# Two value products in every second step: reordering the slots of a cross attention on the matrix engine

## The chip, the core and the metric

The kernel runs on one core of a Trainium2 chip, in one launch. Its matrix engine (TensorE, PE in the profile) writes only to PSUM, eight banks of 512 columns of float32; VectorE (DVE) and ScalarE (ACT) read PSUM, GpSimd (POOL) works on SBUF, and SyncE (SP) issues the transfers. Each engine takes its instructions in the order in which they are written and waits for semaphores. The metric is the device time of one execution in microseconds.

## What is computed

A model of two layers on x of 16 x 64 tokens, width 128. Each layer adds a cross attention to a context of 16 x 1601 keys, a self attention, and a mixture of experts. The change touches the cross attention of layer 1 alone, with 16 heads of width 8:

```
q = split_heads(layernorm(x) @ cq_w + cq_b)
k = split_heads(ctx @ ck_w + ck_b)          # ctx: [16, 1601, 128]
v = split_heads(ctx @ cv_w + cv_b)
scores = einsum('bqhd,bkhd->bhqk', q, k) / sqrt(8) + mask
probs = softmax(scores, axis=-1)
ca = einsum('bhqk,bkhd->bqhd', probs, v)    # goes on to @ co_w and a normalisation
```

All is in float32, and the softmax takes its maximum away before the exponential.

## The kernel before

The cross attention of layer 1 runs in **slots**, one per batch element n, written by `slot` in each engine's block and unrolled by `slots`: n = -2 to 1, a loop of five rounds of two slots, n = 12 to 16. The 1601 keys are 13 **tiles** of 128 (the last has 65), and a slot has 13 **steps**, k = 0 to 12. In a slot PE works on three batch elements at once:

- **Scores** of tile k for n (`scores`, L1371): four matmuls (in the profile `PS<-QB,KS`, 256 columns each) into banks 2 and 3 or 4 and 5 in turn. They wait until the exponential of tile k - 2 has been taken from these banks.
- ScalarE takes the **exponential** (L1174), 128 x 1024, from PSUM into `PT`, which has two halves, used in turn. It waits until the product of tile k - 2 has read its half.
- **Value product** of tile k (`values`, L1356): eight matmuls, each on 32 columns of the array (`tile_position`), four side by side, in float32 (each makes two records in the profile, `PS<-PT,work_area` or `PS<-PT,early`, so 16 records a product). It accumulates in bank 6. In a step, the product of tile k - 1 follows the scores of tile k; that of tile 12 stands at the head of the next slot.
- **Maximum blocks** (`maximum`, L1333; `PS<-KS,QM`): the scores of batch element n + 1, for their maximum alone, with the queries in the rows. There are 26, m0 to m25, mostly one matmul of 512 columns each into bank 0, 1 or 7; VectorE reduces each (L1583) and so frees its bank. The table `UNITS` says in which step and bank each stands. Then PE transposes the negated maximum (`nm`, L1331), and VectorE takes it as two parts, `nmh` and `nml` (L1593, L1594), in step 11.
- **Side items** through bank 7 (`SIDE`, `beside`): the sum of the softmax (`sum`, step 1), value projections v0 to v3 of element n + 1 (steps 2 to 5), key projections k0 to k3 of element n + 2 (steps 6, 7, 11, 12). ScalarE takes each out of bank 7 (L1141, L1152, L1156). v3 is one tile and k3 65 columns; the others are full. `IN_BANK7` is the order of all users of bank 7; each waits until the one before has been taken out.

GpSimd splits the keys in two parts and spreads the queries (L1022, L1037, L1039), and SyncE stacks the parts in `KS` by transfers. A maximum block waits for the last block in its bank to be reduced, and for its stacked keys.

So the order inside a step of before is: scores k, the blocks, value product k - 1, the side item. In step 0 it is: value product 12 of the slot before, the blocks, scores 0. The order is written out by hand; no planner moves it.

Of the kernel before, what the change touches and what calls it, by code (L numbers as in the profile page):

```python
# [53 lines left out]
def build(nc, A, out, scratch, mask_parts):  # L54
    ctx = ExitStack()
    with ctx:
# [86 lines left out]
        with nc.sbuf_tensor("context2", [128, 2 * KT * 128], F32) as context2:  # L143
# [6 lines left out]
        VA = [value_area.rearrange("p (k h c) -> p k h c", k=KT, h=HEADS // 2),  # L150
              early[:, :].rearrange("p (k h c) -> p k h c", k=KT, h=HEADS // 2)]
        PT = sb("PT", [128, 2, 1024])

        mask_sb = PT[0:BATCH, :, :].rearrange("p a n -> p (a n)")[:, 0:KPAD]
        mask_hi, mask_lo = kh[0:BATCH, :], kl[0:BATCH, :]
# [562 lines left out]
        pieces = [[(p, c)] for p in range(8) for c in (0, 1)] + [[(p, 2)] for p in range(8)]  # L718
        pieces += [[(p, 3) for p in range(7)], [(7, 3)]]
        UNITS = []  # L720
        for k, banks in ((12, (0, 1)), (0, (0, 1, 7)), (1, (0, 1)), (2, (0, 1)), (3, (0, 1)), (4, (0, 1)), (5, (0, 1)),
                         (6, (0, 1)), (7, (0, 1)), (8, (0, 1, 7)), (9, (0, 1, 7)), (10, (0,))):
            UNITS += [(k, bk, pieces[len(UNITS) + j]) for j, bk in enumerate(banks)]
        assert len(UNITS) == len(pieces)
        progress("keys_p", [f"k{c}" for c in CS])
        progress("keys_a", [f"kf{c}" for c in CS])
# [85 lines left out]


        SIDE = {1: "sum", 2: "v0", 3: "v1", 4: "v2", 5: "v3", 6: "k0", 7: "k1", 11: "k2", 12: "k3"}
        IN_BANK7 = ["m4", "sum", "v0", "v1", "v2", "v3", "k0", "k1", "m21", "m24", "nm", "k2", "k3"]
        assert [f"m{m}" for m, (k, bk, _) in enumerate(UNITS) if bk == 7] == ["m4", "m21", "m24"]

        def present(item, n):
            c = isinstance(n, int)
# [3 lines left out]
                return not (c and n > 13)  # L823
            return not (c and (n < -1 or n > 14))

        def maxima(n, k):

            c = isinstance(n, int)
            ahead = 2 if k == KT - 1 else 1
            if c and not 0 <= n + ahead < BATCH:  # L830
                return [], None
            return [m for m, unit in enumerate(UNITS) if unit[0] == k], n + ahead

        def side(n, k):

# [252 lines left out]
        def _(act):  # L1088
# [69 lines left out]
            def slot(n, q):  # L1158
                c = isinstance(n, int)
                for k in range(KT):  # L1160
                    if k == 0 and not (c and n < 1):
                        at(S, "pv_p", f"pv{KT - 1}", n - 1)
                        if not (c and n < 2):
                            at(S, "fin_g", "on", n - 2)
                        P["acc_a"].done(S.activation(acc_sb, bank(6, 256), ACT.Copy), "acc")
                    if not (c and (n < 0 or n > 15)):
                        rows = 128 if k < FULL else TAIL
                        par = (k + q) % 2
                        at(S, "exp_p", f"s{k}", n)
                        if k >= 2:  # L1170
                            at(S, "pv_p", f"pv{k - 2}", n)
                        elif not (c and n < 1):
                            at(S, "pv_p", f"pv{k + KT - 2}", n - 1)
                        P["exp_a"].done(S.activation(PT[0:rows, par, :], PS[0:rows, 1024 + 1024 * par:2048 + 1024 * par],  # L1174
                                                     ACT.Exp), f"e{k}")
                    for item in side(n, k):
                        empty(item, n, q)
# [14 lines left out]
        def _(pe):  # L1192
# [163 lines left out]
            def values(n, k, q):  # L1356
                rows = 128 if k < FULL else TAIL
                at(T, "exp_a", f"e{k}", n)
                if k == 0:
                    at(T, "vals_a", "v3", n)  # L1360
                    if not (isinstance(n, int) and n < 1):
                        at(T, "acc_a", "acc", n - 1)
                for r in range(2):
                    for j in range(4):
                        p = 4 * r + j
                        last = mm(PS[32 * j:32 * j + 32, 3072 + 128 * r:3200 + 128 * r], VA[q][0:rows, k, p, :],
                                  PT[0:rows, (k + q) % 2, 128 * p:128 * p + 128], start=k == 0 and r == 0,
                                  stop=k == KT - 1, skip_group_check=True, tile_position=(0, 32 * j))
                P["pv_p"].done(last, f"pv{k}")

# [13 lines left out]

            def slot(n, q):
                live = not (isinstance(n, int) and (n < 0 or n > 15))
                for k in range(KT):
                    units, batch = maxima(n, k)
                    stack = q if k == KT - 1 else 1 - q
                    if k == 0:  # L1390
                        if not (isinstance(n, int) and n < 1):
                            values(n - 1, KT - 1, 1 - q)
                        for m in units:
                            maximum(m, batch, stack, n)
                        if live:
                            scores(n, k, q)
                    else:
                        if live:
                            scores(n, k, q)
                        for m in units:  # L1400
                            maximum(m, batch, stack, n)
                        if k == 11 and present("nm", n):
                            beside("nm", n, q)
                        if live:
                            values(n, k - 1, q)
                    for item in side(n, k):
                        beside(item, n, q)

            slots(pe, slot)

# [326 lines left out]
```

## Time and profile before

| | |
|---|---|
| three runs | 1234.77, 1239.29, 1239.86 us (median 1239.29) |
| the profiled execution | 1236.02 us, span from first to last instruction 1234.2 us |
| slots of layer 1's cross attention in it | from about 405 to 888 us |
| busy over the span: PE, DVE, ACT, POOL | 1022.8, 651.9, 494.8, 345.9 us |
| mean granted clock of TensorE | 0.907 |
| maximum reductions (L1583) | 416, 665 ns each |
| exponentials (L1174) | 208, 1021 ns each |
| the chain that ended last | PE 74%, DVE 14%, ACT 5% of the span |

The shares say which engine to look at; the slots are more than a third of the span, and what bounds them is read there. A row of the timeline gives the start, the time from the first start to the last end of a merged group, and the count. PE's matmuls are pipelined: the record of one block of 512 columns lasts 0.39 us and the next begins sooner. So a price on PE is a distance between starts.

### The profile page before, as it was taken

The numbers are of one execution on the slowest core, as the hardware profiler recorded it, in microseconds if no ns is written. First come the engines' busy times: TensorE is split into PE (matmuls) and PEld (weight loads), VectorE is DVE, ScalarE is ACT, GpSimd is POOL, SyncE is SP. The second block draws the span as 40 slices with busy tenths as digits, with TensorE's granted clock in tenths as the row PEclk, the third lists the DMA queues.
The fourth block names the chain that finished last, engine by engine and source line by source line (L and its number), as shares of the span: only waits on it lengthen the run. The fifth ranks groups of instructions, "written<-read, shape, count | busy, mean of one in ns | idle before, by whom it ended". The sixth has DMA issues, their size and how long they took to land.

```text
span 1234.2 us, 24027 instructions
## 1 busy us (share of the span) xinstructions
PE 1022.8 (83%) x9486; PEld 759.7 (62%) x9486; DVE 651.9 (53%) x1302; ACT 494.8 (40%) x654; POOL 345.9 (28%) x360
## 2 busy tenths in 40 slices
PE   4998684999983799999999999999757633828998
PEld 3676454888861476767777776677535421527897
DVE  3445567444342556666666666666166368655111
ACT  1444153222220156666565665665515101402443
POOL 0200213112203434444444444443131012110110
PEclk9999795999995799999999999999979766957999
DMA  8786001010302554444444444433000000010211
GB/s 251 183 281 258 1 2 51 27 52 27 105 1 51 135 123 118 113 115 119 114 114 113 108 109 121 122 84 83 2 1 2 0 1 0 2 34 1 52 35 35
DMA packets 54250, 96.95 MB, mean 79 GB/s; under 512 B 15704, under 2 KB 31856, under 8 KB 54176
## 3 DMA queue, kind: packets, MB, share of 16 engines
q1 hardware_dynamic: 54176, 95.90, 28.6%
q8 instruction: 54, 0.88, 0.3%
q14 instruction: 20, 0.16, 0.0%
HBM read 40.97 MB, written 13.84 MB: 44 GB/s over the span
## 4 chain that ended last, share of the span: by engine, by line
PE 74%; DVE 14%; ACT 5%; POOL 3%; DMA 2%; issue 2%; SPq 1%; DVEq 0%; ACTq 0%; POOLq 0%
PE PS L261 68%; PE PS L1209 2%; DVE u_all L274 2%; ACT PT L1174 1%; PE PS L353 1%; PE PS L291 1%; POOL rstd_all L280 1%; ACT work_area L403 1%; DVE stats_all L266 1%; PE PS L1242 1%; DVE work_area L452 1%; DVE smax L451 1%; DMA early<-in_ctx 1%; SPq L957 1%; DVE ctxT L274 1%
## 5 line engine op out<-in xcount | busy, mean ns | idle before, releaser
L1583 DVE TENSOR_REDUCE mx<-PS 128x1 f32<-128x512 f32 (+2 forms) x416 | 256.7, 665 | 162.3 <-PE PS L261 161.9
L1174 ACT ACTIVATE PT<-PS 128x1024 f32<-128x1024 f32 (+1 forms) x208 | 210.6, 1021 | 61.5 <-PE PS L261 60.2
L261 PE MATMUL PS<-QB,KS 128*128 128x256 f32 (+1 forms) x832 | 160.7, 319 | 0.3 <-DMA QB<-nml 0.3
L261 PE MATMUL PS<-QB,QS 128*128 128x512 f32 x576 | 150.9, 411 | 1.1 <-POOL QS L568 0.7
L261 PE MATMUL PS<-KS,QM 128*128 128x512 f32 (+1 forms) x512 | 142.8, 379 | 6.5 <-DMA KS<-kl 5.1
L261 PEld LDWEIGHTS PS<-QB,KS 128*128 128x128 f32 (+1 forms) x832 | 115.2, 186 | 35.4 <-issue 24.8
L261 PEld LDWEIGHTS PS<-QB,QS 128*128 128x128 f32 x576 | 106.2, 193 | 32.5 <-DVE PT L653 5.9
L661 DVE SCALAR_TENSOR_TENSOR x<-PS,tok_w,x 128x128 f32<-128x128 f32 x128 | 36.0, 344 | 119.5 <-PE PS L261 119.5
L261 PEld LDWEIGHTS PS<-KS,QM 128*128 128x128 f32 x512 | 80.3, 192 | 26.0 <-issue 13.0
L291 PE MATMUL PS<-consts,u_all 128*128 128x128 f32 x64 | 15.6, 426 | 90.6 <-DVE u_all L274 70.0
L261 PEld LDWEIGHTS PS<-expert_area,work_area 128*128 128x128 f32 (+2 forms) x1000 | 78.8, 171 | 16.5 <-ACT work_area L406 12.0
L261 PE MATMUL PS<-expert_area,work_area 128*128 128x128 f32 (+3 forms) x1000 | 81.0, 255 | 5.8 <-ACT work_area L406 3.3
L640 ACT ACTIVATE work_area<-PS 128x512 f32<-128x512 f32 x64 | 38.3, 598 | 108.6 <-PE PS L261 108.6
L566 POOL TENSOR_TENSOR QS<-expert_area,consts 128x512 fp32r<-128x512 f32 x24 | 25.0, 1040 | 189.8 <-DMA expert_area<-in_L_ffn_experts_w 106.1
L261 PE MATMUL PS<-ctxT,w_L_xattn_ck_w 128*128 128x512 f32 (+1 forms) x128 | 64.0, 584 | 15.7 <-ACT prT L1152 12.2
L1037 POOL TENSOR_TENSOR kh<-prT,consts 128x512 fp32r<-128x512 f32 x32 | 33.6, 1051 | 141.1 <-ACT prT L1152 141.1
L261 PE MATMUL PS<-PT,work_area 128*32 128x128 f32 (+1 forms) x1664 | 67.0, 279 | 3.3 <-ACT PT L1174 3.1
L291 PEld LDWEIGHTS PS<-consts,u_all 128*128 128x128 f32 x64 | 12.6, 224 | 91.9 <-DVE u_all L274 52.7
L261 PE MATMUL PS<-PT,early 128*32 128x128 f32 (+1 forms) x1664 | 67.0, 279 | 2.3 <-ACT PT L1174 2.3
L261 PE MATMUL PS<-w_L_xattn_cv_w,ctxT 128*128 128x128 f32 (+1 forms) x416 | 63.3, 291 | 0.4 <-ACT work_area L1141 0.4
L261 PEld LDWEIGHTS PS<-expert_area,PT 128*128 128x128 f32 x512 | 59.6, 192 | 1.5
L261 PE MATMUL PS<-expert_area,PT 128*128 128x128 f32 x512 | 59.8, 275 | 0.0
(253 smaller groups left out, 1527.5 us busy)
## 6 DMA issues: line engine op xcount, KB each, us to landing
KS<-kh SPq DMA_DIRECT2D x128, 128.0 KB, 2.4
ctxT<-context_transposed SPq DMA_DIRECT2D x16, 800.5 KB, 4.4
context_transposed<-transposed SPq DMA_DIRECT2D x14, 800.5 KB, 10.1
KS<-kh SPq DMA_DIRECT2D x128, 72.1 KB, 2.1
KS<-kl SPq DMA_DIRECT2D x64, 128.0 KB, 2.4
context<-in_ctx SPq DMA_DIRECT2D x8, 768.0 KB
expert_area<-in_L_ffn_experts_w SPq DMA_DIRECT2D x24, 256.0 KB, 3.1
KS<-kl SPq DMA_DIRECT2D x64, 72.1 KB, 2.1
```

Of the source, the lines that this page charges most:

```text
L261: return T.matmul(o, l, r, start=start, stop=stop, **k)
L266: V.bn_stats(stats_all[:, t, :], src[:, t, :]).then_inc(ln_stats, 1)
L274: V.tensor_scalar(dst[:, t, :], src[:, t, :], mv_all[:, t, 0:1], rstd_all[:, t:t + 1], ALU.subtract, ALU.mult).then_inc(ln_xn, 1)
L280: G.tensor_tensor(rstd_all[:, :], var_all[:, :], minus_half.broadcast_to([128, PAIRS]), ALU.pow).then_inc(ln_rstd, 1)
L291: last = T.transpose(PS[:, 512 * (6 + h) + 128 * t:512 * (6 + h) + 128 * t + 128], src[:, 4 * h + t, :], ident)
L566: P[name + "_g"].done(G.tensor_tensor(hi, w[:, j, :], one.broadcast_to([128, FF]), ALU.mult), f"w{2 * k + 1}hi{e}")
L640: ins = S.activation(g_act[:, c % 2, :], bank(2 * (c % 2)), ACT.Silu)
L661: last = V.scalar_tensor_tensor(x[:, 4 * t + q, :], PS[:, 512 * (4 + t) + q * 128:512 * (4 + t) + (q + 1) * 128], tok_w[:, 4 * t + q, e:e ...
L1037: P["keys_g"].done(G.tensor_tensor(kh[:, c0:c0 + cw], src, one.broadcast_to([128, cw]), ALU.mult), f"kh{m}")
L1174: P["exp_a"].done(S.activation(PT[0:rows, par, :], PS[0:rows, 1024 + 1024 * par:2048 + 1024 * par], ACT.Exp), f"e{k}")
L1209: last = T.transpose(PS[:, 512 * (4 + g % 2) + 128 * j:512 * (4 + g % 2) + 128 * j + rows], ctx_nat[n % 4][0:rows, b, k0 + j, :], consts[0 ...
L1583: P["max_v"].done(V.reduce_max(mx[:, p:p + len(parts), c:c + 1], bank(bk, cw * len(parts)).rearrange("q (p k) -> q p k", k=cw), AX), f"m{m}")
```

## The change

`PTS` is a list of three probability buffers: the two halves of `PT`, and 1024 columns of `expert_area` that nothing else uses at that time. The exponential of tile k goes to `PTS[k % 3]` and waits for the product of tile k - 3. The value products of tiles k - 2 and k - 1 are both written in the even step k; the odd steps have none. The blocks get a place within their step: "start" (step 0, behind the product of tile 12), "scores" (behind the scores) or "values" (at the step's end, behind products and side item), and are spread over steps and places anew. In step 12 the side item k3 stands directly behind the scores, ahead of block m0. Number and size of all matmuls, reductions, exponentials and transfers stay.

```
--- before.py
+++ after.py
@@ -150,6 +150,7 @@
         VA = [value_area.rearrange("p (k h c) -> p k h c", k=KT, h=HEADS // 2),
               early[:, :].rearrange("p (k h c) -> p k h c", k=KT, h=HEADS // 2)]
         PT = sb("PT", [128, 2, 1024])
+        PTS = [PT[:, 0, :], PT[:, 1, :], expert_area[:, 2048:3072]]
 
         mask_sb = PT[0:BATCH, :, :].rearrange("p a n -> p (a n)")[:, 0:KPAD]
         mask_hi, mask_lo = kh[0:BATCH, :], kl[0:BATCH, :]
@@ -718,9 +719,13 @@
         pieces = [[(p, c)] for p in range(8) for c in (0, 1)] + [[(p, 2)] for p in range(8)]
         pieces += [[(p, 3) for p in range(7)], [(7, 3)]]
         UNITS = []
-        for k, banks in ((12, (0, 1)), (0, (0, 1, 7)), (1, (0, 1)), (2, (0, 1)), (3, (0, 1)), (4, (0, 1)), (5, (0, 1)),
-                         (6, (0, 1)), (7, (0, 1)), (8, (0, 1, 7)), (9, (0, 1, 7)), (10, (0,))):
-            UNITS += [(k, bk, pieces[len(UNITS) + j]) for j, bk in enumerate(banks)]
+        for k, place, banks in ((12, "scores", (0,)), (0, "start", (1, 0, 7)), (0, "scores", (1,)), (1, "scores", (0,)),
+                                (2, "scores", (1,)), (2, "values", (0, 1)), (3, "scores", (0,)),
+                                (4, "scores", (1,)), (4, "values", (0, 1)), (5, "scores", (0,)),
+                                (6, "scores", (1,)), (6, "values", (0, 1)), (7, "scores", (0,)),
+                                (8, "scores", (1,)), (8, "values", (0, 1, 7)), (9, "scores", (0, 1, 7)),
+                                (10, "scores", (0,))):
+            UNITS += [((k, place), bk, pieces[len(UNITS) + j]) for j, bk in enumerate(banks)]
         assert len(UNITS) == len(pieces)
         progress("keys_p", [f"k{c}" for c in CS])
         progress("keys_a", [f"kf{c}" for c in CS])
@@ -812,8 +817,8 @@
 
 
         SIDE = {1: "sum", 2: "v0", 3: "v1", 4: "v2", 5: "v3", 6: "k0", 7: "k1", 11: "k2", 12: "k3"}
-        IN_BANK7 = ["m4", "sum", "v0", "v1", "v2", "v3", "k0", "k1", "m21", "m24", "nm", "k2", "k3"]
-        assert [f"m{m}" for m, (k, bk, _) in enumerate(UNITS) if bk == 7] == ["m4", "m21", "m24"]
+        IN_BANK7 = ["m3", "sum", "v0", "v1", "v2", "v3", "k0", "k1", "m21", "m24", "nm", "k2", "k3"]
+        assert [f"m{m}" for m, (k, bk, _) in enumerate(UNITS) if bk == 7] == ["m3", "m21", "m24"]
 
         def present(item, n):
             c = isinstance(n, int)
@@ -823,13 +828,13 @@
                 return not (c and n > 13)
             return not (c and (n < -1 or n > 14))
 
-        def maxima(n, k):
+        def maxima(n, k, place=None):
 
             c = isinstance(n, int)
             ahead = 2 if k == KT - 1 else 1
             if c and not 0 <= n + ahead < BATCH:
                 return [], None
-            return [m for m, unit in enumerate(UNITS) if unit[0] == k], n + ahead
+            return [m for m, unit in enumerate(UNITS) if unit[0][0] == k and place in (None, unit[0][1])], n + ahead
 
         def side(n, k):
 
@@ -1167,11 +1172,11 @@
                         rows = 128 if k < FULL else TAIL
                         par = (k + q) % 2
                         at(S, "exp_p", f"s{k}", n)
-                        if k >= 2:
-                            at(S, "pv_p", f"pv{k - 2}", n)
+                        if k >= 3:
+                            at(S, "pv_p", f"pv{k - 3}", n)
                         elif not (c and n < 1):
-                            at(S, "pv_p", f"pv{k + KT - 2}", n - 1)
-                        P["exp_a"].done(S.activation(PT[0:rows, par, :], PS[0:rows, 1024 + 1024 * par:2048 + 1024 * par],
+                            at(S, "pv_p", f"pv{KT - 1}", n - 1)
+                        P["exp_a"].done(S.activation(PTS[k % 3][0:rows, :], PS[0:rows, 1024 + 1024 * par:2048 + 1024 * par],
                                                      ACT.Exp), f"e{k}")
                     for item in side(n, k):
                         empty(item, n, q)
@@ -1364,7 +1369,7 @@
                     for j in range(4):
                         p = 4 * r + j
                         last = mm(PS[32 * j:32 * j + 32, 3072 + 128 * r:3200 + 128 * r], VA[q][0:rows, k, p, :],
-                                  PT[0:rows, (k + q) % 2, 128 * p:128 * p + 128], start=k == 0 and r == 0,
+                                  PTS[k % 3][0:rows, 128 * p:128 * p + 128], start=k == 0 and r == 0,
                                   stop=k == KT - 1, skip_group_check=True, tile_position=(0, 32 * j))
                 P["pv_p"].done(last, f"pv{k}")
 
@@ -1384,27 +1389,33 @@
 
             def slot(n, q):
                 live = not (isinstance(n, int) and (n < 0 or n > 15))
+
+
+                def block_maxima(k, place):
+                    units, batch = maxima(n, k, place)
+                    for m in units:
+                        maximum(m, batch, q if k == KT - 1 else 1 - q, n)
+
                 for k in range(KT):
-                    units, batch = maxima(n, k)
-                    stack = q if k == KT - 1 else 1 - q
                     if k == 0:
                         if not (isinstance(n, int) and n < 1):
                             values(n - 1, KT - 1, 1 - q)
-                        for m in units:
-                            maximum(m, batch, stack, n)
-                        if live:
-                            scores(n, k, q)
-                    else:
-                        if live:
-                            scores(n, k, q)
-                        for m in units:
-                            maximum(m, batch, stack, n)
-                        if k == 11 and present("nm", n):
-                            beside("nm", n, q)
-                        if live:
-                            values(n, k - 1, q)
-                    for item in side(n, k):
-                        beside(item, n, q)
+                        block_maxima(k, "start")
+                    if live:
+                        scores(n, k, q)
+                    if k == KT - 1:
+                        for item in side(n, k):
+                            beside(item, n, q)
+                    block_maxima(k, "scores")
+                    if k == 11 and present("nm", n):
+                        beside("nm", n, q)
+                    if live and k and k % 2 == 0:
+                        values(n, k - 2, q)
+                        values(n, k - 1, q)
+                    if k < KT - 1:
+                        for item in side(n, k):
+                            beside(item, n, q)
+                    block_maxima(k, "values")
 
             slots(pe, slot)
```

What PE does around steps 2 and 3 (names: `QB,KS` scores, `KS,QM` blocks, `PT` or `expert_area` with `work_area` products, `w_L_xattn_cv_w` value projections), before:

```order
L261 MATMUL PS<-QB,KS 128x256 x4
L261 MATMUL PS<-KS,QM 128x512 x2
L261 MATMUL PS<-PT,work_area 32x128 x8
L261 MATMUL PS<-w_L_xattn_cv_w,ctxT 128x128 x4
L261 MATMUL PS<-QB,KS 128x256 x4
L261 MATMUL PS<-KS,QM 128x512 x2
L261 MATMUL PS<-PT,work_area 32x128 x8
L261 MATMUL PS<-w_L_xattn_cv_w,ctxT 128x128 x4
```

and after:

```order
L262 MATMUL PS<-QB,KS 128x256 x4
L262 MATMUL PS<-KS,QM 128x512
L262 MATMUL PS<-PT,work_area 32x128 x16
L262 MATMUL PS<-w_L_xattn_cv_w,ctxT 128x128 x4
L262 MATMUL PS<-KS,QM 128x512 x2
L262 MATMUL PS<-QB,KS 128x256 x4
L262 MATMUL PS<-KS,QM 128x512
L262 MATMUL PS<-w_L_xattn_cv_w,ctxT 128x128 x4
```

Both products are in step 2 now. Two blocks (7 in bank 0, 8 in bank 1) end it, and block 9, in bank 0 again, comes one score tile later.

PE from step 8 to the transpose of step 11 (the block with 66 columns x7 is m24), before:

```order
L261 MATMUL PS<-QB,KS 128x256 x4
L261 MATMUL PS<-KS,QM 128x512 x3
L261 MATMUL PS<-PT,work_area 32x128 x8
L261 MATMUL PS<-QB,KS 128x256 x4
L261 MATMUL PS<-KS,QM 128x512 x2
L261 MATMUL PS<-KS,QM 128x66 x7
L261 MATMUL PS<-PT,work_area 32x128 x8
L261 MATMUL PS<-QB,KS 128x256 x4
L261 MATMUL PS<-KS,QM 128x66
L261 MATMUL PS<-PT,work_area 32x128 x8
L261 MATMUL PS<-QB,KS 128x256 x4
L1331 MATMUL PS<-consts,nm 8x128
```

and after, from step 8 as well:

```order
L262 MATMUL PS<-QB,KS 128x256 x4
L262 MATMUL PS<-KS,QM 128x512
L262 MATMUL PS<-PT,work_area 32x128 x16
L262 MATMUL PS<-KS,QM 128x512 x3
L262 MATMUL PS<-QB,KS 128x256 x4
L262 MATMUL PS<-KS,QM 128x512 x2
L262 MATMUL PS<-KS,QM 128x66 x7
L262 MATMUL PS<-QB,KS 128x256 x4
L262 MATMUL PS<-KS,QM 128x66
```

Blocks 19 to 24 stand with nothing but one score tile between them.

PE from the transpose of step 11 into the next slot, after (`ctxT,w_L_xattn_ck_w` are key projections k2 and k3):

```order
L1336 MATMUL PS<-consts,nm 8x128
L262 MATMUL PS<-ctxT,w_L_xattn_ck_w 128x512
L262 MATMUL PS<-QB,KS 65x256 x4
L262 MATMUL PS<-ctxT,w_L_xattn_ck_w 128x65
L262 MATMUL PS<-KS,QM 128x512
L262 MATMUL PS<-PT,work_area 32x128 x8
L262 MATMUL PS<-expert_area,work_area 32x128 x8
L262 MATMUL PS<-PT,work_area 32x128 x8
L262 MATMUL PS<-KS,QM 128x512 x3
L262 MATMUL PS<-QB,KS 128x256 x4
L262 MATMUL PS<-KS,QM 128x512
```

Before, a product stood between the transpose and k2, and two blocks and a product between the scores of tile 12 and k3. Now the products of tiles 10, 11 and 12 are neighbours.

## Rows read from the trace of the kernel before

**Rows 1.** Busy time by stretches: before slot 0, two neighbouring slots (from `nm` to `nm`).

```profile
core 0: us, PE busy (x) PEld busy (x) DVE busy (x) ACT busy (x) POOL busy (x), PEclk, DMA share, GB/s
405.00:434.00 29.00, 24.56 (x79) 14.94 (x79) 19.66 (x34) 6.04 (x10) 12.74 (x14) 0.74 0.57 138
603.72:633.25 29.53, 28.95 (x332) 20.68 (x329) 18.51 (x31) 17.76 (x23) 14.13 (x19) 1.00 0.45 113
633.25:662.42 29.17, 28.89 (x331) 20.61 (x329) 18.50 (x31) 17.77 (x23) 14.08 (x19) 1.00 0.46 114
```

**Rows 2.** Timeline of PE, one full step; start, length, engine, line, names, count.

```profile
614.64 0.72 PE L261 MATMUL PS<-QB,KS 128*128 128x256 f32 x4
615.20 0.63 PE L261 MATMUL PS<-KS,QM 128*128 128x512 f32 x2
615.76 0.64 PE L261 MATMUL PS<-PT,work_area 128*32 128x128 f32 x16
616.34 1.16 PE L261 MATMUL PS<-w_L_xattn_cv_w,ctxT 128*128 128x128 f32 x8
617.25 0.71 PE L261 MATMUL PS<-QB,KS 128*128 128x256 f32 x4
```

**Rows 3.** Timeline of PE, heads of two slots, in narrow windows.

```profile
461.55 0.97 PE L261 MATMUL PS<-KS,QM 128*128 128x512 f32 x3
462.35 1.10 PE L261 MATMUL PS<-QB,KS 128*128 128x256 f32 x8
463.29 0.63 PE L261 MATMUL PS<-KS,QM 128*128 128x512 f32 x2
464.09 0.42 PE L261 MATMUL PS<-PT,early 128*32 128x128 f32 x8 [0.17 <-ACT PT L1174]
...
608.52 0.40 PE L261 MATMUL PS<-KS,QM 128*128 128x512 f32 x1
...
608.76 0.39 PE L261 MATMUL PS<-KS,QM 128*128 128x512 f32 x1
```

**Rows 4.** Timeline of PE, one value product, in two windows.

```profile
613.16 0.43 PE L261 MATMUL PS<-PT,work_area 128*32 128x128 f32 x8
...
613.16 0.64 PE L261 MATMUL PS<-PT,work_area 128*32 128x128 f32 x16
```

**Rows 5.** Timeline of DVE, the reduction of the block at 615.20.

```profile
615.63 0.69 DVE L1583 TENSOR_REDUCE mx<-PS 128x1 f32<-128x512 f32 x1 [0.44 <-PE PS L261]
```

**Rows 6.** Timeline ahead of slot 0, reductions of DVE, weight loads of PE behind them.

```profile
422.09 3.76 DVE L1583 TENSOR_REDUCE mx<-PS 128x1 f32<-128x512 f32 x7 [0.62 <-PE PS L261]
...
423.43 0.19 PEld L261 LDWEIGHTS PS<-KS,QM 128*128 128x128 f32 x1 [0.35 <-DVE mx L1583]
424.03 0.97 PEld L261 LDWEIGHTS PS<-KS,QM 128*128 128x128 f32 x8 [0.41 <-DVE mx L1583]
```

**Rows 7.** Timeline of steps 11 and 12, all engines.

```profile
603.72 0.27 PE L1331 MATMUL PS<-consts,nm 128*8 128x128 f32 x1
...
604.35 0.28 DVE L1594 TENSOR_TENSOR nml<-PS,nmh 8x128 fp32r<-8x128 f32 x1
...
604.68 1.12 PE L261 MATMUL PS<-ctxT,w_L_xattn_ck_w 128*128 128x512 f32 x2
...
605.92 0.69 ACT L1152 ACTIVATE prT<-PS,c_L_xattn_ck_b 128x512 f32<-128x512 f32 x1 [0.98 <-PE PS L261]
...
606.11 0.63 PE L261 MATMUL PS<-KS,QM 128*128 128x512 f32 x2
```

**Rows 8.** Timeline at a slot's head, ACT and PE.

```profile
609.74 1.94 ACT L1174 ACTIVATE PT<-PS 128x1024 f32<-128x1024 f32 x2 [0.95 <-PE PS L261]
...
609.93 0.63 PE L261 MATMUL PS<-KS,QM 128*128 128x512 f32 x2
...
611.03 0.64 PE L261 MATMUL PS<-PT,work_area 128*32 128x128 f32 x16 [0.47 <-ACT PT L1174]
```

**Rows 9.** Timeline of PE, step 8.

```profile
627.42 1.04 PE L261 MATMUL PS<-KS,QM 128*128 128x512 f32 x3
...
628.39 0.64 PE L261 MATMUL PS<-PT,work_area 128*32 128x128 f32 x16
```

## Prediction, made before the changed kernel ran

> **What bounds the kernel now.** I read the busy time of each engine by stretches first. The 16 slots of layer 1's cross attention take two lengths in turn, 29.53 and 29.17 us, mean 29.35, with the matrix engine (PE) busy 28.95 and 28.89 us of them at a granted clock of 1.00; VectorE is busy 18.5 and ScalarE 17.8 us [rows 1]. So PE bounds a slot, and only PE's own time, or a wait that PE meets, counts. Next I read PE alone in order of time, to get the price of each item by the distance from start to start (records overlap, so their lengths are too long). Then the places where PE stands next to another engine: banks handed over by VectorE, the chain of the negated maximum, the first exponential of a slot.
>
> **Prices.** Eight score matmul records, two key tiles, take 462.35 to 463.29: 0.47 us per tile. Two maximum blocks start 608.52 and 608.76: 0.23 each [rows 3]. A full step from 614.64 to 617.25 holds one score tile, two blocks, one value product and a value projection of 0.91 (616.34 to 617.25), in 2.61 us. So a lone value product costs 2.61 - 0.47 - 0.46 - 0.91 = 0.77 [rows 2]. Inside one, the first 8 records span 0.43 and all 16 span 0.64, so eight more take 0.21 and sixteen 0.43 [rows 4]. A second product directly behind the first therefore costs 0.43, and a lone one carries 0.34 of change-over. Where a block or side item had to wait, its weight load is no longer hidden: three blocks after a change-over take 461.55 to 462.35 = 0.80, not 0.69 [rows 3]; I price this exposed load at 0.11.
>
> The hand-over of a bank: block at 615.20, its reduction at 615.63, so 0.43 later, for 0.69 [rows 2, 5]. Queued reductions end 0.60 apart (PE's reloads behind them stand at 423.43 and 424.03). The reductions started 422.09, the second thus ends 422.09 + 0.60 + 0.69 = 423.38, and the load that needed it came at 423.43: 0.06 [rows 6]. So a bank can be written again 0.43 + 0.69 + 0.06 = 1.18 after its block, and the new block then moves 0.11 later, at 1.29; the third bank of three adjacent blocks at 1.29 + 1.20 = 2.49.
>
> **Part 1: products together.** Before there are 13 lone value products a slot. After, six runs: tiles 0 and 1, 2 and 3, up to 8 and 9, and then 10, 11 and 12, because the one at the next slot's head follows directly. Seven change-overs go. Six of them are worth 6 x 0.34 = 2.04. The seventh is not a gain. Tile 10's product stood between the transpose of the negated maximum (603.72) and key projection k2 (604.68), and k2 waits for VectorE's second half of that maximum, which starts 604.35 and lasts 0.28 [rows 7]. The chain takes these 0.96 us whatever PE does meanwhile, so 0.77 of work was almost free there, and without it the time stays. Now the product is paid elsewhere: +0.43. Behind the waiting k2 all later items of the slot are queued on PE.
>
> **Part 2: waits that go.** The product of tile 0 waited for the first exponential: 609.93 to 611.03 is 1.10 for two blocks and the change-over, which take 0.56 at 615.20 to 615.76, so 0.54 of waiting; in the other kind of slot 463.29 to 464.09 is 0.80, so 0.24 [rows 2, 3, 8]. Mean 0.39. It now stands a step later, with tile 1's exponential behind it on ScalarE (two in 1.94 us, 609.74 to 611.68), and the sum, a score tile and a block before it: gone. The bank-7 block of step 8 waited for key evacuation: 627.42 to 628.39 is 0.97 for three blocks and a change-over, 0.79 unhindered, so 0.18 [rows 9]; it now stands behind two products: gone. The third probability buffer costs nothing and is needed: the exponential of tile k overwrites tile k-3, whose product ran before its scores were queued.
>
> **Part 3: waits that come.** All are in the new order of blocks and sides.
> - Steps 3, 5 and 7 begin with scores and then a block in bank 0, whose last block (7, 11, 15) ended the step before. Between the two starts PE has two blocks and a score tile, 0.46 + 0.47 = 0.93; the bank is good at 1.29. Waiting 0.36 each, 1.08. Before, a value product and a side item lay between.
> - Blocks 19, 20, 21, one score tile, 22, 23, 24: the products that lay between are gone. Block 24 would start 5 x 0.23 + 0.47 = 1.62 after 19, its bank is good at 2.49: 0.87 for the three.
> - Blocks 1, 2, 3 at the slot's head, then scores, 4, scores, 5, sum. The sum would start 0.69 + 0.47 + 0.23 + 0.47 + 0.23 = 2.09 after block 1, and needs bank 7, good at 2.49: 0.40 (block 4 takes part of the same).
> - k3 now follows the scores directly and needs bank 7 from k2. k2 starts 604.68, ScalarE takes it at 605.92 for 0.69, end 606.61, that is 1.93, with 0.06 and 0.11: 2.10. The scores are over at 606.11, 1.43 after [rows 7]. Waiting 0.67. Blocks 0 and 1 and tile 11's product covered this before. Queued behind: block 0, three products.
>
> Sum: 1.08 + 0.87 + 0.40 + 0.67 = 3.02. None of these is in the trace of before as such; their bounds are nothing (if something I count as idle turns out to be filled) and these values plus 0.11 each.
>
> The Trainium skill, TensorEngine Tiling (PSUM Bottleneck), says that tiling speeds TensorE but not the evacuation of PSUM. That speaks against this change, and by it the sum would stand on the side of the 3.02, as my rows put it.
>
> **Sum.** A slot: -2.04 + 0.43 - 0.39 - 0.18 + 3.02 = +0.84. Thirteen slots (1 to 13) have all of it: +10.9. Slot 0 has no sum item: +0.4. Slots 14 and 15 have no key projections, the last no blocks either, so merging pays and little waits: -1.2 for both, an estimate. Ahead of slot 0, with no scores to cover them, the three waits in bank 0 can be 0.36 + 0.47 = 0.83 each, against waits that stand there already: 0 to 2.5, I take 1.5. Total +11.6. Everything behind the slots is untouched. The profiled execution took 1236.0 us (span 1234.2), so 1247.6; the median of the runs, 1239.3, stands 3.3 above it, by which it is 1250.9. I take 1249.
>
> **Rivals.**
> *The merging pays and the waits stay away (faster).* Only the gains of parts 1 and 2 come: -2.18 a slot, over 14 slots -30.5, so 1208. For it: in before PE shows hardly a wait for VectorE, and VectorE has 11 us of idle time in a slot. Against: it is the distance of two blocks in one bank that counts, and for blocks 7 and 9 that shrinks from a whole step of 2.6 us to 0.93. It decides if a bank is free again within 0.93 of its block instead of 1.18. The Trainium skill, TensorEngine Tiling (Key Properties), says that changing the tiling mode drains the engine; my 0.34 is that drain, and by that rule alone seven would go at 2.4 us a slot.
> *Even.* Only the exposed loads are my error: without 0.11 on six waits (three in bank 0, 24, the sum, k3) a slot gains 0.66 back, 13 x 0.66 = 8.6: 1239 by the profile, 1242 by the median. The rows show this load after a change-over and in a few waits, not in these.
> *The clock.* In the 29 us ahead of slot 0, where PE waits for banks, the mean granted clock was 0.74 (stretches at 1.2 GHz) [rows 1]. A mean of 0.74 over 29 us is 15 us at the lower level, and each such stretch among the slots, where PE bounds, would cost 15 x 0.5 = 7.5. The new order puts 3 us of waits into each slot, but spread in pieces under 1 us, and none of the waits of before inside the slots went with a fall. Two such stretches: 1264.
> *The pair does not run as a run* (0.77 for the second product too): +0.84 + 2.04 a slot, 1275. Rows inside one product speak against it.
>
> **Chances.** Forecast 0.56 (1243 to 1257), even 0.20, faster 0.17, the clock or no run 0.07. The range leaves out the faster rival and the far end: 1230 to 1262. About 0.5% (6 us) is what a measurement of this kernel can tell from no change: faster 0.17, same 0.22, slower 0.61.
>
> **What would show it.** Slots of 30.2 us with the alternation smaller. In PE's order: 0.64 + 0.43 for a pair of products, then the side item. PE waiting for VectorE's reductions about seven times a slot, near nothing before; a key projection k2 0.96 behind the transpose with nothing between; k3 waiting 0.6 for ScalarE; no wait before the product of tile 0. If slots are shorter than 29.2, the banks come free earlier than 1.18 behind their block, or the blocks are further apart than I count, and the forecast is wrong at part 3.

## The result, and the profile after

The changed kernel takes 1254.2 us in the median of four runs (1251.8 to 1255.89), the kernel before 1239.57 (1234.77 to 1240.93): a ratio of 1.0124, 95% interval 1.009 to 1.0157. So it is slower by 15 us. Forecast was 1249 with 1243 to 1257 around it, from a sum of 12 us. The profiled execution of the changed kernel took 1255.6 us, its span is 1253.8.

Where the time came in is read by stretches, cut at the first maximum block and at the transposes `nm` in step 11, from one to the next. First the kernel before, then the changed one (columns as in [rows 1]):

```profile
405.02:426.21 21.19, 18.28 (x64) 11.27 (x65) 16.18 (x27) 3.76 (x7) 7.83 (x9) 0.80 0.52 132
426.21:457.01 30.80, 29.15 (x275) 20.23 (x276) 16.88 (x29) 16.35 (x20) 11.57 (x11) 0.89 0.49 120
457.01:838.14 381.13, 375.83 (x4279) 268.18 (x4277) 240.59 (x403) 230.92 (x299) 181.59 (x223) 1.00 0.46 112
838.14:865.96 27.82, 27.31 (x328) 19.85 (x325) 18.50 (x31) 16.61 (x21) 7.85 (x10) 1.00 0.36 82
865.96:887.79 21.83, 19.22 (x317) 13.63 (x315) 2.32 (x4) 16.41 (x18) 2.21 (x4) 1.00 0.01 3
887.79:1234.20 346.41, 232.62 (x1874) 182.16 (x1874) 170.60 (x383) 90.28 (x113) 55.21 (x42) 0.81 0.06 14
```

```profile
406.13:428.41 22.28, 17.50 (x63) 10.53 (x63) 16.32 (x27) 3.44 (x6) 7.94 (x8) 0.81 0.50 128
428.41:460.54 32.13, 29.80 (x275) 21.86 (x276) 17.15 (x29) 16.68 (x20) 11.65 (x11) 0.84 0.48 118
460.54:856.44 395.90, 376.18 (x4280) 284.55 (x4277) 239.13 (x403) 230.84 (x299) 181.04 (x223) 1.00 0.44 108
856.44:885.04 28.60, 27.18 (x327) 21.08 (x325) 18.39 (x31) 16.50 (x21) 7.42 (x10) 1.00 0.31 70
885.04:905.83 20.79, 18.43 (x317) 13.37 (x315) 2.32 (x4) 15.53 (x18) 2.20 (x4) 1.00 0.01 3
905.83:1253.80 347.97, 234.40 (x1874) 183.88 (x1874) 170.64 (x383) 90.31 (x113) 55.21 (x42) 0.81 0.06 14
```

The third row is thirteen slots: 381.13 to 395.90, or 29.32 to 30.45 us a slot, +1.14. Neighbouring slots, 29.53 and 29.17 before, are now 30.51 and 30.47: the alternation is nearly gone (forecast: smaller). PE was busy 375.83 before and 376.18 now, VectorE and ScalarE the same to 1.5 us: no engine got more work, PE stands still longer. (Weight loads, PEld, are as many and last longer in sum, 268.18 to 284.55.) The two stretches ahead add 2.4, the two behind take 0.3 away. In the second row, with slot 0, the granted clock was 0.89 before and 0.84 after, so PE was some 3.5 us longer at its lower level there (an estimate from the two means); how much of that row's 1.3 us is clock and how much waits is not separated. The part behind the slots (346.41 to 347.97) and the part ahead of the first block (405.02 to 406.13) are other work and differ by 2.7 together, which is what single executions differ by; so this trace shows 19.6 where the medians show 15.

Whom PE waits for in the thirteen slots, changed kernel (us in total, times, longest):

```profile
PEld PS L262 <- DVE mx L1594: 28.1, 91, 0.4
PEld PS L262 <- DVE nml L1605: 12.9, 13, 1.1
PE PS L262 <- DVE nml L1605: 9.2, 13, 0.8
PEld PS L262 <- ACT prT L1157: 8.2, 13, 0.7
PE PS L262 <- ACT prT L1157: 4.9, 13, 0.4
PEld PS L262 <- ACT expert_area L1179: 2.4, 10, 0.2
```

and the kernel before:

```profile
PEld PS L261 <- ACT PT L1174: 14.0, 54, 0.5
PEld PS L261 <- DVE nml L1594: 5.2, 13, 0.5
PEld PS L261 <- ACT keys_f L1152: 4.4, 13, 0.4
PE PS L261 <- ACT PT L1174: 3.6, 13, 0.5
PEld PS L261 <- DVE mx L1583: 1.6, 8, 0.2
```

91 waits for a reduction are seven a slot, as forecast; 8 in all before. The waits for an exponential (`PT`, now also `expert_area`) are nearly gone, 17.6 us in 67 waits before and 2.6 in 11 now; so are the 13 for key evacuation at step 8 (`keys_f`). 13 for k2's evacuation (`prT`) came, and the wait for the second half of the maximum (`nml`) is longer, because no product covers it.

The steps themselves, changed kernel. Products and blocks of steps 2 and 3, PE's timeline (answers to [rows 2]):

```profile
621.88 1.08 PE L262 MATMUL PS<-PT,work_area 128*32 128x128 f32 x32
622.89 1.16 PE L262 MATMUL PS<-w_L_xattn_cv_w,ctxT 128*128 128x128 f32 x8
623.80 0.70 PE L262 MATMUL PS<-KS,QM 128*128 128x512 f32 x2
624.35 0.64 PE L262 MATMUL PS<-QB,KS 128*128 128x256 f32 x4
625.06 0.50 PE L262 MATMUL PS<-KS,QM 128*128 128x512 f32 x1
```

From the start of the pair to the projection is 1.01, where a lone product took 0.58 [rows 2]: the second costs 0.43 and no change-over. Then the score tile at 624.35 is followed by block 9 only at 625.06, 0.71 later and not 0.47, and the block's record has 0.50 and not 0.39: it waited, and its weight load was not hidden.

Blocks 19 to 24, all engines (answers to [rows 6], in a slot now):

```profile
637.80 0.97 PE L262 MATMUL PS<-KS,QM 128*128 128x512 f32 x3
...
639.68 0.19 PEld L262 LDWEIGHTS PS<-KS,QM 128*128 128x128 f32 x1 [0.41 <-DVE mx L1594]
...
640.28 0.86 PEld L262 LDWEIGHTS PS<-KS,QM 128*128 128x128 f32 x7 [0.41 <-DVE mx L1594]
```

Block 24 starts 2.48 behind block 19; forecast was 2.49 where PE alone would need 1.62. The loads come 0.60 apart, VectorE's rhythm.

Steps 11 and 12 (answers to [rows 7]):

```profile
612.84 0.27 PE L1336 MATMUL PS<-consts,nm 128*8 128x128 f32 x1
...
613.46 0.28 DVE L1605 TENSOR_TENSOR nml<-PS,nmh 8x128 fp32r<-8x128 f32 x1
...
613.80 1.13 PE L262 MATMUL PS<-ctxT,w_L_xattn_ck_w 128*128 128x512 f32 x2 [0.69 <-DVE nml L1605]
...
615.04 0.69 ACT L1157 ACTIVATE prT<-PS,c_L_xattn_ck_b 128x512 f32<-128x512 f32 x1 [0.98 <-PE PS L262]
...
615.78 0.44 PE L262 MATMUL PS<-ctxT,w_L_xattn_ck_w 128*128 128x65 f32 x2 [0.40 <-ACT prT L1157]
...
616.16 0.49 PE L262 MATMUL PS<-KS,QM 128*128 128x512 f32 x1
...
616.58 0.64 PE L262 MATMUL PS<-PT,early 128*32 128x128 f32 x16
```

The transpose to k2 is 0.96 with nothing between, as it was with a product between [rows 7]. k3 comes 1.98 behind k2. One thing was not counted: block 0, now behind k3, lasts 0.42 to the product, and a block with its change-over 0.33 elsewhere.

### The profile page after: what moved, and what is told of

It reads as the page before. It is cut to its first block, busy times and chain, and to the rows that moved or that the text cites. A ratio compares the mean times of both kernels' runs of the same rounds, so it can differ in the third digit from the quotient of the medians.

```text
span 1253.8 us, 24026 instructions
## 1 busy us (share of the span) xinstructions
PE 1024.2 (82%) x9486; PEld 781.1 (62%) x9486; DVE 652.6 (52%) x1302; ACT 494.1 (39%) x654; POOL 345.4 (28%) x360
## 4 chain that ended last, share of the span: by engine, by line
PE 69%; DVE 19%; ACT 5%; issue 2%; POOL 2%; DMA 2%; SPq 1%; DVEq 0%; ACTq 0%
PE PS L262 63%; DVE mx L1594 5%; PE PS L1214 2%; DVE u_all L275 2%; PE PS L354 1%; PE PS L292 1%; POOL rstd_all L281 1%; ACT work_area L404 1%; PE PS L1247 1%; DVE stats_all L267 1%; ACT prT L1157 1%; DVE work_area L453 1%; DVE smax L452 1%; DMA early<-in_ctx 1%; SPq L962 1%
## 5 line engine op out<-in xcount | busy, mean ns | idle before, releaser
L262 PE MATMUL PS<-KS,QM 128*128 128x512 f32 (+1 forms) x512 | 179.3, 418 | 13.2 <-DVE mx L1594 3.5
L1179 ACT ACTIVATE PT<-PS 128x1024 f32<-128x1024 f32 x144 | 145.4, 1022 | 71.9 <-PE PS L262 70.6
L262 PE MATMUL PS<-QB,KS 128*128 128x256 f32 (+1 forms) x832 | 151.9, 306 | 0.9 <-DMA QB<-nml 0.7
L262 PEld LDWEIGHTS PS<-QB,KS 128*128 128x128 f32 (+1 forms) x832 | 121.4, 187 | 28.0 <-issue 15.7
L262 PEld LDWEIGHTS PS<-KS,QM 128*128 128x128 f32 x512 | 85.5, 193 | 55.5 <-DVE mx L1594 36.1
L262 PE MATMUL PS<-expert_area,work_area 128*128 128x128 f32 (+4 forms) x1512 | 101.3, 262 | 5.8 <-ACT work_area L407 3.3
L262 PEld LDWEIGHTS PS<-expert_area,work_area 128*128 128x128 f32 (+3 forms) x1512 | 92.1, 150 | 19.1 <-ACT work_area L407 12.0
L262 PE MATMUL PS<-ctxT,w_L_xattn_ck_w 128*128 128x512 f32 (+1 forms) x128 | 63.0, 576 | 30.1 <-ACT prT L1157 18.7
L1179 ACT ACTIVATE expert_area<-PS 128x1024 f32<-128x1024 f32 x64 | 65.5, 1023 | 16.5 <-PE PS L262 16.4
L262 PE MATMUL PS<-w_L_xattn_cv_w,ctxT 128*128 128x128 f32 (+1 forms) x416 | 60.7, 285 | 0.5 <-ACT work_area L1146 0.5
L262 PEld LDWEIGHTS PS<-w_L_xattn_cv_w,ctxT 128*128 128x128 f32 (+1 forms) x416 | 53.2, 190 | 9.0 <-issue 5.8
```

The lines of the kernel that those rows point to most:

```text
L262: return T.matmul(o, l, r, start=start, stop=stop, **k)
L1179: P["exp_a"].done(S.activation(PTS[k % 3][0:rows, :], PS[0:rows, 1024 + 1024 * par:2048 + 1024 * par], ACT.Exp), f"e{k}")
```

## The experiments

All were timed beside the kernel before. The order inside a step is written here as the list of what PE does: S scores, m blocks (in the places of the table), P a value product with its tile, side a side item, nm the transpose. Ratios are against the kernel before, whose medians beside them were 1238.1, 1236.4 and 1236.3 us in the three groups of four.

### Single moves taken back

**k3 behind the products.**

```
-step 12: S, side (k3), m, P10, P11
+step 12: S, m, P10, P11, side (k3)
```

> The changed kernel with one item moved: in step 12 the key projection k3 stands behind block m0 and the products of tiles 10 and 11 again, so that the product of tile 12 is parted from them. Theory (PE meets waits of known price): the wait of 0.67 us for bank 7 is covered and goes, one change-over of 0.31 comes back: -0.36 us in each of 13 slots, and the same wait goes ahead of slot 0, so 5 us less than the changed kernel, some 1249, slots of 30.1. Rival (the loss is the work of the pairs and the third buffer, the waits are covered by each other): the freed wait turns up at the next item, the time stays within 1 us or rises by the change-over (+4).

Measured: 1246.2 us, ratio 1.0056 (1.0035 to 1.0077), so 8 us less than the changed kernel (5 forecast). Slots take 29.96 us, 0.49 less than 30.45; the theory had 0.36. Besides the 0.67 the 0.09 at block 0 went. The waits for `prT` are gone from the list. The rival falls: nothing turned up at the next item.

**Tile 10's product behind the transpose.**

```
-step 11: S, nm, side (k2)
-step 12: S, side (k3), m, P10, P11
+step 11: S, nm, P10, side (k2)
+step 12: S, side (k3), m, P11
```

> The changed kernel with one product moved: tile 10's stands behind the transpose of the negated maximum in step 11 again, ahead of key projection k2; 8 and 9 stay a pair, 11 and 12 are one. Theory (the stretch from transpose to k2 lasts 0.96 us, filled or not): the product costs nothing there and its 0.46 in the run goes, the number of change-overs outside the stretch stays: -0.46 x 13 = 6 us less than the changed kernel, some 1248. Rival (k2's start is not set by the maximum's two parts but by PE's own queue): the product adds itself to the stretch, 0.77 - 0.46 = +0.31 a slot, 4 us more.

Measured: 1250.1 us, ratio 1.0085 (1.0062 to 1.0109), 4 us less where 6 were forecast. This interval overlaps that of the changed kernel (1.009 to 1.0157), so the gain rests on the slots of the two traces: 30.05 us, 0.41 less. Of PE's waits in the thirteen slots of this kernel, the row for the maximum's second half is

```profile
PEld PS L262 <- DVE nml L1596: 5.2, 13, 0.5
```

5.2 us as before and not 12.9. So a product of 0.77 is nearly free behind the transpose and costs 0.4 in a run: the gain that a merge promised is a loss at this place.

**The blocks of steps 2 to 7 apart.**

```
-steps 2, 4, 6: S, m (bank 1), P, P, side, m (banks 0, 1);  steps 3, 5, 7: S, m (bank 0), side
+steps 2, 4, 6: S, m (bank 1), P, P, side, m (bank 0);      steps 3, 5, 7: S, m (bank 1), side, m (bank 0)
```

> The changed kernel with the blocks of steps 2 to 7 laid out anew: one in bank 1 behind the scores and one in bank 0 at the end of every step, so that two in one bank always have a side item or products between them. Theory: the three waits of 0.36 for VectorE go; one short wait for the reciprocals (0.17), and one of 0.2 at k1, which follows k0 sooner, come; with what turns up elsewhere 0.5 us a slot less, -6 to -8 in all, some 1247. Rival (no bank wait matters): no change, 1254.

Measured: 1245.4 us, ratio 1.0057 (1.004 to 1.0074), 8 us less than the changed kernel. Slots of 29.85 us, 0.60 less. The waits for reductions fall from 28.1 us to

```profile
PEld PS L262 <- DVE mx L1585: 16.9, 52, 0.4
```

Three a slot are gone (91 to 52). They were priced at 1.08, and 0.60 came back as gain; twelve waits for key evacuation are new (2.8 us in all).

**Tile 8's product between blocks 21 and 22.**

```
-step 9: S, m (22, 23, 24);      step 10: S, m, P8, P9
+step 9: S, P8, m (22, 23, 24);  step 10: S, m, P9
```

> The changed kernel with tile 8's product alone in step 9 between blocks 19-21 and 22-24, and 9's alone in step 10. Theory: of the 0.87 us that blocks 22 to 24 wait, all but 0.1 is covered by a product of 0.77; one change-over of 0.31 comes: -0.46 a slot, 6 us less than the changed kernel, some 1248. Rival (products together are what pays or costs, waits are spurious): +0.31 a slot, 4 us more.

Measured: 1248.0 us, ratio 1.0073 (1.0056 to 1.0089), slots of 30.01 us, 0.44 less against 0.46. A pair taken apart made the kernel faster, because the half of it covers the reductions.

### The two halves of the change alone

**Products together, blocks as before**, with three buffers:

```
-steps k = 1 to 12: S, m, (nm), P(k-1), side
+even steps:        S, m, P(k-2), P(k-1), side
+odd steps:         S, m, (nm), side
```

> The kernel before with its blocks and side items where they were, three probability buffers, and the products of two tiles in every second step. Theory: five change-overs go (0.31 each, 1.55; tile 12's stays apart behind k3), the waits ahead of tile 0's product and at block 21 shrink (0.4); tile 10's product leaves the covered stretch (0.77 of cover gone, net +0.46) and small bank waits of 1.1 us come in steps 1, 2, 6 and 7: -0.3 a slot, 4 to 6 us less than the kernel before, some 1233. Rival (the pairs cost the time, not the block order): slower than before, as the changed kernel is, 1250.

Measured: 1231.2 us, ratio 0.9958 (0.9936 to 0.998), slots of 29.16 us against 29.32. Faster by 5 us, as expected. Eleven of the thirteen slots take 28.97 to 29.03, the expected 0.3 less; the second and third take 30.03 and 29.94, and only there PE waits for stacked keys (`KS<-kl`, 0.7 us at most), which the theory had not. The pairs are not what costs, but they bring little by themselves.

**Blocks and k3 as in the changed kernel, one product a step:**

```
-even steps: S, m, P(k-2), P(k-1), side, m;  odd steps: S, m, side
+even steps: S, m, P(k-1), side, m;          odd steps: S, m, P(k-1), side
+step 12: S, side (k3), m, P11
```

> The changed kernel's blocks and its k3 directly behind the scores, with three buffers, but one product in every step as in before. Theory: the bank waits of the new block order stay (about 2.3 us a slot), the wait at k3 (0.67) too, and all change-overs are paid: about 2 us a slot over before, 1265 to 1272. Rival (products together are what costs): the time of before, 1239.

Measured: 1273.6 us, ratio 1.0293 (1.0266 to 1.0321), the slowest of all, with slots of 31.52 us. The expected 1265 to 1272 was 2 us short. The whole loss, and more, is in where the blocks and k3 stand. The two halves do not add: 2.20 a slot for the blocks and -0.16 for the pairs would make 2.04, the changed kernel has 1.14. On top of the new block order the merging takes 1.07 a slot off, on top of the old one 0.16.

**Three buffers alone**, the order of before:

```
-P["exp_a"].done(S.activation(PT[0:rows, par, :], ...
+P["exp_a"].done(S.activation(PTS[k % 3][0:rows, :], ...
```

> The kernel before with three probability buffers alone, one product a step and all else as it was. Theory: ScalarE never waited for a buffer, so nothing: within 1 us of before. Rival (writing a third of the exponentials to the other area costs or frees something): 3 us or more either way.

Measured: 1236.6 us, ratio 1.0002 (0.9985 to 1.0018), slots of 29.30 us. Nothing, as expected.

### The cause of the bank waits

The same reduction over half the columns, in the changed kernel and in the kernel before:

```
 P["max_v"].done(V.reduce_max(mx[:, p:p + len(parts), c:c + 1],
-                             bank(...).rearrange("q (p k) -> q p k", k=cw), AX), f"m{m}")
+                             bank(...).rearrange("q (p k) -> q p k", k=cw)[:, :, 0:min(cw, 256)], AX), f"m{m}")
```

> The changed kernel, but VectorE reduces only the first 256 of the 512 columns of a maximum block (so the maximum is that of half the keys, and the result is another); PE's work and order stay. A reduction should last 0.42 us instead of 0.69. Theory (PE waits for banks that VectorE gives back too late): the waits of blocks 9, 13, 17 shrink by 0.27 each, those of blocks 22 to 24 and of the sum nearly vanish: 1.9 us a slot, 25 to 28 us in all, some 1227, below the kernel before; the 0.67 at k3 and the 0.96 at k2 stay. Rival (the stalls are PE's own, at each change of tile shape, or ScalarE's): the same time as the changed kernel, 1254.

> The control: the kernel before with the same half reductions (the maximum is that of half the keys). Theory: PE does not wait for VectorE in its slots, so only the stretch ahead of slot 0 gains, 1 to 3 us: some 1236. Rival (a shorter reduction helps everywhere, so the test above shows nothing of the new order): 20 us or more.

Measured: the changed kernel 1220.5 us, ratio 0.9881 (0.9851 to 0.9911); the kernel before 1234.2, ratio 0.9986 (0.997 to 1.0001). So shorter reductions, with PE's work and order untouched, take 30 us (by the ratios) off the one and 2, hardly clear of nothing, off the other. The theory had 25 to 28 and 1 to 3. The control's slots stay at 29.34 us. The reductions in the changed kernel's thirteen slots, and its PE around block 9:

```profile
L1594 DVE TENSOR_REDUCE mx<-PS 128x1 f32<-128x256 f32 (+1 forms) x338 | 131.9, 418 | 189.9 <-PE PS L262 187.8
```

```profile
606.73 0.70 PE L262 MATMUL PS<-KS,QM 128*128 128x512 f32 x2
607.27 0.64 PE L262 MATMUL PS<-QB,KS 128*128 128x256 f32 x4
607.75 0.48 PE L262 MATMUL PS<-KS,QM 128*128 128x512 f32 x1
```

A reduction lasts 418 ns; block 9 stands 0.48 behind the score tile, not 0.71, and still with part of its weight load exposed (0.48 of record). Slots take 28.47 us, 0.85 less than before, and no wait for a reduction is in the list; those for `nml` (12.9 us) and `prT` (8.2) are as in the changed kernel. With the bank waits gone the pairs pay, though not the full 2.18 a slot of parts 1 and 2: k3 still waits 0.67, and the change-overs were worth less than priced (below).

PE's busy time in the thirteen slots falls from 376.18 to 356.07 us here, with the same matmuls. So busy time of PE holds waits too; it does not tell its work.

### Putting it together

**All four moves back**, on the changed kernel:

```
+steps 2 to 7: blocks as in "apart"
+step 9: S, P8, m;  step 10: S, m, P9;  step 11: S, nm, P10, side;  step 12: S, m, P11, side
```

> The changed kernel with the four single edits together: k3 behind the products, tile 10's product behind the transpose, blocks of steps 2 to 7 apart, tile 8's product between blocks 21 and 22. Theory (the prices add): the four measured apart sum to about 25 us less than the changed kernel, walking through a slot with the prices gives 24: 9 us less than before, some 1229. Rival (they cover each other): as good as the best single one, 1245.

Measured: 1226.1 us, ratio 0.9919 (0.9894 to 0.9944), slots of 28.68 us, 1.78 less than the changed kernel's. The single ones give 0.49 + 0.41 + 0.60 + 0.44 = 1.94. They nearly add.

**The blocks placed by the prices**, four pairs, P10 behind the transpose, P11 ahead of k3:

```
 0: P12, m(7), S, m(1), side            1: S, m(0), side, m(1)
 2: S, P0, P1, side                     3: m(0), S, m(1), side
 4: S, m(0,1), P2, P3, side, m(0)       5: m(1), S, side
 6: S, m(0,1), P4, P5, m(0), side, m(1) 7: S, m(0), side
 8: S, m(1,0), P6, P7, m(7)             9: m(1), S, m(0)
10: S, m(7,1,0), P8, P9                11: S, nm, P10, side
12: S, m(0,1), P11, side, m(0)          (banks of the blocks in brackets)
```

> Products as in the pairs with tile 10's behind the transpose and 11's ahead of k3, and the 26 blocks placed so that, by the prices read off the trace (block 0.23, score tile 0.47, product 0.77 alone and 0.46 behind another, bank good 1.18 after its block), almost no wait is left: no sum wait, no wait of blocks 9, 13, 17, 22 to 24. Theory: a slot of 27.6 to 27.9 us, 1.6 less than before, 25 us in all, some 1213. Rival (blocks placed earlier wait for stacked keys or spread queries, which I have no price for): half of that, 1225, with PE waiting for transfers.

Measured: 1210.7 us (1210.3 to 1211.6), ratio 0.9791 (0.9766 to 0.9815). Its thirteen slots, and a piece of its PE:

```profile
458.56:816.97 358.41, 356.48 (x4279) 276.56 (x4277) 247.20 (x403) 227.35 (x299) 181.08 (x223) 1.00 0.48 120
```

```profile
604.49 1.08 PE L262 MATMUL PS<-PT,work_area 128*32 128x128 f32 x32
605.50 1.16 PE L262 MATMUL PS<-w_L_xattn_cv_w,ctxT 128*128 128x128 f32 x8
606.42 0.47 PE L262 MATMUL PS<-KS,QM 128*128 128x512 f32 x1
606.73 0.63 PE L262 MATMUL PS<-QB,KS 128*128 128x256 f32 x4
607.20 0.39 PE L262 MATMUL PS<-KS,QM 128*128 128x512 f32 x1
607.43 1.07 PE L262 MATMUL PS<-w_L_xattn_cv_w,ctxT 128*128 128x128 f32 x8
```

27.57 us a slot, PE busy in 356.48 of 358.41, no wait for a reduction left in the list of waits. Two neighbouring blocks are in different banks, and the next in the same bank is 1.38 us away or more in the slot of this piece, with one exception: block 6 stands 1.17 behind block 4 (603.52 and 602.35), and its record has 0.57 and not 0.39, so its load is not hidden. The rival (blocks that come earlier wait for transfers) falls: PE waits for one in all thirteen slots, for 0.2 us.

**Two products behind the transpose**, tiles 9 and 10, with 8 alone and the blocks placed once more:

```
-10: S, m(7,1,0), P8, P9;  11: S, nm, P10, side
+10: S, m(7,1,0), P8;      11: S, nm, P9, P10, side
```

> Like the kernel with searched block places, but two products (tiles 9 and 10) stand behind the transpose, 8 alone in step 10, and the blocks are placed anew. Theory: 0.77 + 0.46 = 1.23 of work in a stretch of 0.96 hides nearly all of the chain of the maximum, 0.2 a slot less than one product there: 27.5 us a slot, 2 to 3 us less in all, some 1208. Rival (the chain's end is already covered): the same, 1211.

Measured: 1207.3 us (1206.8 to 1208.2), ratio 0.9767 (0.974 to 0.9794), slots of 27.28 us. It is the fastest, 29 us below the kernel before beside it; that it beats the one above is likely from the slots (0.29 us each), while the intervals of the two ratios overlap.

## Why the prediction was right, and where it was off

- **What bounds** stood: PE's order, not any engine's work. In every kernel here PE's granted clock in the thirteen slots was 1.00, also at 31.5 us a slot. The clock rival, which put falls among the slots, fell.
- **Waits that come** (3.02 a slot) came place by place: block 24 at 2.48 behind block 19 for 2.49; block 9 waits 0.24 and shows its load, 0.35 for 0.36; k2 0.96 behind the transpose for 0.96; k3 1.98 behind k2, 0.55 more than its scores need, and the load for the rest. The half reductions show that the bank waits are VectorE's.
- **The rival "even"** fell at its own point: the exposed load of a block that waited is there (0.50 of record against 0.39).
- **The merge was sized too well.** A slot grew by 1.14, not by 0.84. The pair itself was priced right: unrounded the second product costs 0.44 for the 0.43 of [rows 4], and up to 0.46 in the run of three (616.58 to block 1 at 618.08), 0.1 a slot in all. What failed is the one price of 0.34 for every change-over. The product of tile 8 stood between block 24, whose matmuls have 66 columns, and a score tile. PE there, before and after:

```profile
630.02 0.86 PE L261 MATMUL PS<-KS,QM 128*128 128x66 f32 x7
630.81 0.64 PE L261 MATMUL PS<-PT,work_area 128*32 128x128 f32 x16
631.39 0.74 PE L261 MATMUL PS<-QB,KS 128*128 128x256 f32 x4
631.97 0.19 PE L261 MATMUL PS<-KS,QM 128*128 128x66 f32 x1
...
640.28 0.97 PE L262 MATMUL PS<-KS,QM 128*128 128x66 f32 x7
641.09 0.72 PE L262 MATMUL PS<-QB,KS 128*128 128x256 f32 x4
641.64 0.19 PE L262 MATMUL PS<-KS,QM 128*128 128x66 f32 x1
```

  From block 24 to block 25 it is 1.95 with the product and 1.36 without. It cost 0.59 there and not 0.77, so taking it into a pair (0.44) saved 0.15 and not 0.34. With the 0.09 at block 0, which I had not counted, these terms are some 0.37 too low together. Against them stand 0.11, a load counted twice: block 19 is now directly behind a product, its load is not hidden (0.34 to block 20, not 0.23), and this is in the price of the change-over and in the 0.87 as well. That makes 0.26 of the missing 0.30; the rest is not traced. No run shows either that the 0.34 is a drain of the engine, as the prediction calls it; the traces give its price at two places and no cause.
- **Waits that go** stood, nearly: what is left of the waits for an exponential is 2.6 us in thirteen slots, and none stands ahead of the product of tile 0.
- **Ahead of slot 0** the stretches grew by 2.4, forecast 1.9; some of it may be the clock, as said above. **Slots 14 and 15** lost 0.3, not 1.2: slot 14 still has all its blocks and their waits (27.82 to 28.60), only the last gained (21.83 to 20.79). That was an estimate without rows, and its sign for slot 14 was wrong.
- By the trace the slots and the stretches ahead add 16.9 us where the sum had 11.6. The medians grew by 14.6, and 1243 to 1257 was wide enough for that.
- The rival "the merging pays and the waits stay away" names what half reductions brought about, at 1220 us and not its 1208, as k3's wait stays. Its condition, a bank that is free when PE comes back, is the right one: with half reductions block 9 starts 1.02 behind block 7 (606.73 to 607.75), and the reduction of block 7, from 607.25 for 0.42, is over at 607.67.

## What to carry over

When a step is merged to save change-overs, list what the parts used to cover before counting the gain: here each lone product was also the time in which another engine emptied a bank, and one of them was nearly free because it stood in a chain of VectorE. Price the change-over where it stands: it was 0.33 with full blocks ahead of the product and 0.15 behind the 66-column block. Two users of one bank need a distance on PE of at least the block's latency plus the reduction plus the hand-over (here 1.2 to 1.3 us); with that one number and the price of each item, an order can be judged on paper, and the best one found so took 2.3% off. A stretch in which an engine must wait anyway is where lone work belongs.

## What the runs showed that I had not expected

A sum of start-to-start prices carries further than I had thought, into orders that no trace had shown. From the expectations above, slots of 29.0, 30.0, 30.0 and 30.1 us were to be expected of the pairs alone, of tile 10's and tile 8's products taken back, and of k3 behind the products; they measured 29.16, 30.05, 30.01 and 29.96. Beyond their bounds came the blocks alone (1273.6 us for at most 1272), the half reductions (30 us for at most 28) and, by hundredths, the first order placed by prices (slots of 27.57 for at least 27.6).

An exposed weight load is not all or nothing: block 9 behind a wait of 0.24 has a record of 0.50 us, with nearly no wait (half reductions) still 0.48, and without any 0.39. The traces suggest why: where the bank has long been free, the block's load starts 0.12 ahead of it (602.92 for the block at 603.04, placed by the prices); with half reductions it starts at 607.73 for 607.75, 0.06 behind the end of the reduction at 607.67. So the bank came free just too late to hide the load, by less than the list of waits shows. No run varied this alone.
